# Attention on one core: the maximum and the bias of each head's exponential made by one two-source VectorE operation

## The chip, the cores and the metric

The kernel runs on one core of one Trainium2 chip, as a single launch. The metric is the device time of that launch in microseconds (us); less is better. One more execution was recorded by the hardware profiler, and all rows below come from it.

## What is computed

The reference runs two blocks over 8 sequences of 128 tokens with 256 features (8 tiles of 128 tokens). A first layer has a small cross-attention and a feed-forward part with ternary weights. The second layer is a cross-attention over 16 heads of 16 features with rounded operands, and a second feed-forward part. The change lies in the second layer's cross-attention, which in the reference reads:

```
q = _fq_sym(q, axis=-1)            # per token and head: s = max|q| / 127, at least 1e-8; q = round(q / s) * s
k = _fq_sym(k, axis=-1)
v = _fq_sym(v, axis=2)
attn = jnp.einsum('bhqd,bhkd->bhqk', q, k)     # 1024 keys for each query
attn = jax.nn.softmax(attn, axis=-1)
attn = _fq_unsigned(attn, axis=-1)             # round to 255 steps of the row's largest
out = jnp.einsum('bhqk,bhkd->bhqd', attn, v)
```

Since the row's largest softmax value becomes 255, the kernel needs only exp(s * (score - max score) + ln 255), rounded to an integer, and its sum. Here `score` is the product of the rounded query integers with the keys, and `s` is that query's scale.

## The kernel before

It is written engine by engine, with semaphores by hand; the order of the work on each engine is the order of the calls in the code. The attention of the second layer is a loop over 128 units (`U = T * H`, a token tile `t` and a head `h`). In each unit `u`:

- TensorE: `scores(u)` writes 128x1024 scores to two banks of PSUM. There are three such slots, so it waits until ScalarE has done unit u-3 (`s_exp`).
- VectorE: `attention(u)` takes the negated maximum of the 1024 scores of each row into `nm`, a ring of three (L1472).
- GpSimd: `bias(u)` computes `eb = nm * sq + ln 255` on 128x1 values (L658). `sq` holds the scales of the queries.
- ScalarE: `attention(u)` runs the exponential over the same two banks with bias `eb` and scale `sq`, writes 128x1024 integers and gives their sum through its accumulator (L992).
- The integers are turned by a DMA, or for 4 heads of 16 (from the second tile on) by TensorE with a ScalarE copy (`move`, L979), and then TensorE multiplies them with the values (L2062), some 7 units later.

Between these, VectorE does work that comes once in a tile (reciprocal of the sums L1448, scaling L1453, residual L1460) and work that comes once in two tiles, the layer norm and rounding of two finished tiles (L1127 to L1274, L1464). GpSimd has other work in the same loop: layer-norm roots, `x2_bp`, `x3_b2`, and `b1_part`, 28 pieces for the feed-forward part, one behind each bias from unit 36 on. `quantise_rows` makes the integers and scales of the queries; it is called four times by `q_quant4`, twice before unit 0 and twice between units 4 and 9.

## Time and profile before

| what | value |
|---|---|
| median of 3 runs | 398.39 us (395.93 to 398.97) |
| profiled execution | 397.65 us, its span from the first to the last instruction 395.8 us |
| granted TensorE clock, mean of the profiled execution | 0.888 |
| VectorE busy | 85% of the span |
| ScalarE busy | 80% of the span |
| TensorE matmul busy | 77% of the span |
| GpSimd busy | 39% of the span |

The time of an execution and the span of its instructions differ by 1.85 us here. The shares are averages over stages with different limits; the attention lies between 151 and 343 us of the span.

### The profile page before, as it was taken

Reading aid. Unit: us, or ns where it says so; the run is one execution under the profiler, and the core shown is the slowest. Engines: PE = TensorE matmul, PEld = TensorE weight load, DVE = VectorE, ACT = ScalarE, POOL = GpSimd, SP = SyncE. Lnnn points to the kernel's source line nnn. Section 1 sums busy time; section 2 is a strip of 40 time slices with the busy share of each in tenths; the row PEclk is TensorE's granted clock in tenths of the full one; section 3 lists DMA queues with packets and bytes.
Section 4 is the critical chain, followed back from the end, with each engine's and each line's share of the span. In section 5 each row is a group of like instructions: output and inputs, shape, how many; then the busy total and the mean of one; then the engine's idle time right before and its main releaser. Section 6 shows DMA issues by size and latency. Waiting matters only on the chain.

```text
span 395.8 us, 7466 instructions
## 1 busy us (share of the span) xinstructions
PE 304.7 (77%) x2557; PEld 190.7 (48%) x2589; DVE 334.7 (85%) x542; ACT 316.8 (80%) x517; POOL 153.9 (39%) x324
## 2 busy tenths in 40 slices
PE   7989999767696996667677768666767757777966
PEld 6656565422585883333444434434444434433433
DVE  4648998868788879878998999999999999598786
ACT  3766789967345688788999989999999999887852
POOL 6423525469740423104224565413122233156330
PEclk9969999899699899865998988999899998985578
DMA  8900013500300015959999998999898988600001
GB/s 265 393 3 3 0 61 104 208 2 0 106 0 2 1 27 104 136 106 162 181 167 166 169 166 140 161 174 172 161 173 141 170 122 153 101 0 17 13 27 55
DMA packets 126342, 42.68 MB, mean 108 GB/s; under 512 B 121056, under 2 KB 124768, under 8 KB 125536
## 3 DMA queue, kind: packets, MB, share of 16 engines
q1 hardware_dynamic: 125872, 41.60, 54.4%
q8 instruction: 21, 0.34, 0.4%
q0 software_dynamic: 144, 0.52, 0.3%
q14 instruction: 17, 0.14, 0.1%
q10 hardware_dynamic: 288, 0.07, 0.1%
HBM read 11.24 MB, written 1.05 MB: 31 GB/s over the span
## 4 chain that ended last, share of the span: by engine, by line
PE 33%; DVE 21%; ACT 21%; issue 16%; POOL 6%; DMA 1%; SPq 0%; ACTq 0%; DVEq 0%; POOLq 0%
ACT rb L992 15%; PE ps L2035 4%; DVE nm L1472 4%; PE ps L1940 4%; PE ps L2140 3%; PE ps L1944 2%; PE ps L2047 2%; PE ps L2097 2%; PE ps L2011 2%; PE ps L1913 2%; DVE st L1127 1%; PE ps L2106 1%; PE ps L2095 1%; POOL ra L558 1%; POOL ra L559 1%
## 5 line engine op out<-in xcount | busy, mean ns | idle before, releaser
L1472 DVE TENSOR_REDUCE nm<-ps 128x1 f32<-128x1024 f32 x128 | 153.3, 1218 | 11.5 <-PE ps L2035 10.8
L992 ACT ACTIVATE rb<-ps,eb,sq 128x1024 int16<-128x1024 f32 x128 | 153.6, 1212 | 9.3 <-POOL eb L658 8.7
L2035 PE MATMUL ps<-ra,rb 128*128 128x512 bf16 x229 | 80.0, 426 | 49.1 <-ACT rb L992 46.7
L658 POOL TENSOR_SCALAR eb<-nm,sq 128x1 f32<-128x1 f32 x128 | 34.2, 267 | 120.0 <-DVE nm L1472 118.9
L2035 PEld LDWEIGHTS ps<-ra,rb 128*128 128x128 bf16 x256 | 16.1, 101 | 63.6 <-ACT rb L992 60.9
L2062 PEld LDWEIGHTS ps<-ra,tern 128*128 128x128 f16 x624 | 25.5, 98 | 17.9 <-issue 7.2
L2062 PE MATMUL ps<-ra,tern 128*128 128x16 f16 x624 | 25.9, 171 | 2.7 <-DVE rb L1202 2.7
L992 ACT ACTIVATION_READ_ACCUMULATOR rb<-ps,eb,sq 128x1 f32 x128 | 26.7, 209 | 0.0
L2047 PEld LDWEIGHTS ps<-idh,rb 128*128 128x128 f16 x224 | 15.9, 107 | 14.5 <-issue 10.4
L2047 PE MATMUL ps<-idh,rb 128*128 128x128 f16 x224 | 19.3, 236 | 3.6 <-issue 2.2
L1913 PE MATMUL ps<-xqT,tern 128*128 128x512 bf16 x62 | 16.6, 397 | 6.3 <-DVE rb L1382 4.9
L2062 PEld LDWEIGHTS ps<-ra,stage 128*128 128x128 f16 x400 | 16.5, 98 | 10.1 <-issue 3.8
L1940 PE MATMUL ps<-h,ra 128*128 128x256 f32 x64 | 16.8, 429 | 3.4 <-POOL ra L559 3.4
L855 ACT ACTIVATE sB<-ps,shift,small 128x1024 uint8<-128x1024 f32 x8 | 9.7, 1208 | 9.1 <-DVE small L1420 9.0
L2062 PE MATMUL ps<-ra,stage 128*128 128x16 f16 x400 | 16.7, 171 | 0.0
L1940 PEld LDWEIGHTS ps<-h,ra 128*128 128x128 f32 x64 | 13.8, 219 | 5.7 <-issue 3.4
L1372 DVE TENSOR_TENSOR gs<-ps,sB 128x512 f32<-128x512 f32 x16 | 11.0, 688 | 6.1 <-PE ps L1913 4.4
L848 ACT ACTIVATE sl<-gs 128x512 f32<-128x512 f32 x16 | 9.8, 624 | 7.2 <-DVE rb L1382 5.7
L1418 DVE TENSOR_REDUCE small<-ps 128x1 f32<-128x1024 f32 x8 | 9.8, 1221 | 5.5 <-PE ps L1940 3.0
L599 POOL TENSOR_SCALAR small<-small 128x1 f32<-128x1 f32 x8 | 6.5, 811 | 20.2 <-DVE small L1420 20.2
L775 ACT ACTIVATE wint<-stage,wrec 128x2048 int16<-128x2048 f32 x5 | 10.0, 1998 | 5.3 <-DVE tern L1235 4.3
L1913 PEld LDWEIGHTS ps<-xqT,tern 128*128 128x128 bf16 x64 | 5.5, 100 | 15.5 <-DVE rb L1382 7.5
(242 smaller groups left out, 716.6 us busy)
## 6 DMA issues: line engine op xcount, KB each, us to landing
stage<-w SPq DMA_DIRECT2D x2, 1024.0 KB, 6.7
rb<-ra SPq DMA_DIRECT2D x16, 128.0 KB, 3.1
xs<-x SPq DMA_DIRECT2D x4, 256.0 KB, 4.2
cx<-ctx_in SPq DMA_DIRECT2D x4, 256.0 KB, 4.4
stage<-w_gate SPq DMA_DIRECT2D x1, 1024.0 KB, 7.9
stage<-w_up SPq DMA_DIRECT2D x1, 1024.0 KB, 11.1
stage<-w_down SPq DMA_DIRECT2D x1, 1024.0 KB, 4.8
cx<-wide_rows SPq DMA_DIRECT2D x1, 1024.0 KB, 6.4
```

What stands on the lines that cost most here:

```text
L658: nc.gpsimd.tensor_scalar(eb[:, u % 3:u % 3 + 1], nm[:, u % 3:u % 3 + 1], sq[:, t, h:h + 1], LN255, ALU.mult, ALU.add).then_inc(s_bias, 1)
L775: A(wint[:, :], wslot(i), ACT.Identity, scale=wrec[:, i:i + 1]).then_inc(w_int, 1)
L848: A(sl[:, n % 2, :], gs[:, n % 2, :], ACT.Silu).then_inc(g_silu, 1)
L992: A(esc[u % E_RING], bank(2 * (u % 3), 2), ACT.Exp, bias=eb[:, u % 3:u % 3 + 1], scale=sq[:, t, h:h + 1], accum_out=es[:, t % 2, h:h + 1]) ...
L1372: V.tensor_tensor(gs[:, n % 2, :], bank(GATE_UP_BANKS[n][0]), sB[:, 512 * hf:512 * hf + 512], ALU.mult).then_inc(g_scaled, 1)
L1472: V.tensor_reduce(nm[:, u % 3:u % 3 + 1], bank(2 * (u % 3), 2), AX.X, ALU.max, negate=True).then_inc(s_max, 1)
L1913: ins = M(bank(b), tern[:, w, F * k + P * c:F * k + P * c + P], xqT[:, k, 512 * hf:512 * hf + 512], start=(k == 0), stop=(k == 1))
L1940: ins = M(y[:, 2 * P * c:2 * P * c + 2 * P], m[:, 4 * k + c, :], h128[:, P * k:P * k + 2 * P], start=(k == 0), stop=(k == 1))
L2035: ins = M(bank(2 * (u % 3) + hf), qz[t % 2][:, h // 2, h % 2, :], kT[:, h // 2, 512 * hf:512 * hf + 512], start=True, stop=True)
L2047: ins = TR(half_bank(7)[:, P * c:P * c + P], esc[u % E_RING].bitcast(F16)[:, P * c:P * c + P], idh[:, :])
L2062: ins = M(bank(6)[:, HD * h:HD * h + HD], rT[u % R_RING][:, P * c:P * c + P], vq[:, c, HD * h:HD * h + HD], start=(c == 0), stop=(c == T - 1))
L2140: ins = M(b, fT16[:, t % 2, P * c:P * c + P], w[:, D * c:D * c + D], start=False, stop=(c == FC - 1))
```

## The change

One VectorE operation with two sources and an accumulator takes the place of the maximum on VectorE and the step on GpSimd. It computes (score - ln 255 / s) * (-s) for every score, writes these 1024 values as bf16 to memory that nothing reads (`unread`, three places in free buffers), and keeps their minimum, which is -s * max + ln 255: the bias itself. The two per-row numbers that it needs, `sqn = -s` and `sql = -ln 255 / s`, come from `quantise_rows`, which makes them for each query. The second source is `sql` broadcast along the row. `eb` becomes a ring of four, and VectorE waits for the exponential of unit u-4 before it writes it. The semaphore `s_max` and the tile `nm` go.

```diff
-            def bias(u):
-                t, h = divmod(u, H)
-                pool.wait_ge(s_max, u + 1)
-
-                nc.gpsimd.tensor_scalar(eb[:, u % 3:u % 3 + 1], nm[:, u % 3:u % 3 + 1], sq[:, t, h:h + 1],
-                                        LN255, ALU.mult, ALU.add).then_inc(s_bias, 1)
-
             for u in range(U + 3):
-                if u < U:
-                    bias(u)
...
-            def quantise_rows(psum, bias, factor, scale, out_i):
+            def quantise_rows(psum, bias, factor, scale, negative, shifts, out_i):
...
-                link(V.tensor_scalar(scale, ka[:, :], factor / 127.0, QMIN, ALU.mult, ALU.max))
-                link(V.reciprocal(kr[:, :], scale))
-                if factor != 1.0:
-                    link(V.tensor_scalar(kr[:, :], kr[:, :], factor, None, ALU.mult))
+                link(V.tensor_scalar(ks[:, :], ka[:, :], 1.0 / 127.0, QMIN / factor, ALU.mult, ALU.max))
+                V.tensor_scalar(scale, ks[:, :], factor, None, ALU.mult)
+                V.tensor_scalar(negative, ks[:, :], -factor, None, ALU.mult)
+                link(V.reciprocal(kr[:, :], ks[:, :]))
+                V.tensor_scalar(shifts, kr[:, :], -LN255 / factor, None, ALU.mult)
...
             def attention(u):
                 if u < U:
+                    t, h = divmod(u, H)
+                    if h == 0:
+                        dve.wait_ge(q_int, t // 2 + 1)
                     dve.wait_ge(s_ps, u + 1)
-                    if u >= 3:
-                        dve.wait_ge(s_bias, u - 2)
-                    V.tensor_reduce(nm[:, u % 3:u % 3 + 1], bank(2 * (u % 3), 2), AX.X, ALU.max,
-                                    negate=True).then_inc(s_max, 1)
+                    if u >= 4:
+                        dve.wait_ge(s_exp, u - 3)
+
+                    V.tensor_tensor_reduce(out=unread[u % 3], in0=bank(2 * (u % 3), 2), in1=sql[:, t, h:h + 1].to_broadcast([P, NK]),
+                                           scale=sqn[:, t, h:h + 1], scalar=3.0e38, op0=ALU.add, op1=ALU.min,
+                                           accum_out=eb[:, u % 4:u % 4 + 1]).then_inc(s_bias, 1)
```

VectorE's queue in the middle of the attention, around the layer norm of a finished pair of tiles, before (`nm` is the negated maximum, `ps` the scores):

```order
L1472 TENSOR_REDUCE nm<-ps 128x1 [waits s_bias,s_ps] x2
L1127 BN_STATS st<-xs 128x6 [waits x3_done]
L1127 BN_STATS st<-xs 128x6
L1130 BN_AGGR mv<-st 128x2 [waits dve_link]
L1130 BN_AGGR mv<-st 128x2
L1472 TENSOR_REDUCE nm<-ps 128x1 [waits s_bias,s_ps] x2
```

The same place after (the line numbers of the changed file differ; `stage` and `gs` are the unread outputs, `eb` the bias):

```order
L1470 ISA gs,eb<-ps,sql,sqn 128x1024 [waits s_exp,s_ps]
L1470 ISA eb 128x1
L1470 ISA stage,eb<-ps,sql,sqn 128x1024 [waits s_exp,s_ps,q_int]
L1470 ISA eb 128x1
L1120 BN_STATS st<-xs 128x6 [waits x3_done]
L1120 BN_STATS st<-xs 128x6
L1123 BN_AGGR mv<-st 128x2 [waits dve_link]
L1123 BN_AGGR mv<-st 128x2
L1470 ISA stage,eb<-ps,sql,sqn 128x1024 [waits s_exp,s_ps]
L1470 ISA eb 128x1
```

Every unit is now two instructions on VectorE: the pass over 128x1024, and a second one that writes the accumulator to `eb`. Nothing else there changed its place; VectorE's queue has 128 instructions more for the units.

GpSimd's queue from unit 32 on, where the pieces of `b1_part` (`wint`) begin, before:

```order
L658 TENSOR_SCALAR eb<-nm,sq 128x1 [waits s_max] x17
L616 TENSOR_TENSOR x<-xs,row 128x256 [waits x3_done]
L658 TENSOR_SCALAR eb<-nm,sq 128x1 [waits s_max] x3
L625 CAST wint<-wkvs 128x256 [waits w_tern,ld_wide]
L658 TENSOR_SCALAR eb<-nm,sq 128x1 [waits s_max,pool_link]
L627 TENSOR_SCALAR wint<-wint,col 128x256
L658 TENSOR_SCALAR eb<-nm,sq 128x1 [waits s_max,pool_link]
L629 TENSOR_TENSOR wint<-wkvs,wint 128x256
```

A later stretch of the same work after:

```order
L627 CAST wint<-wkvs 128x256 [waits w_tern,ld_wide]
L629 TENSOR_SCALAR wint<-wint,col 128x256 [waits pool_link]
L631 TENSOR_TENSOR wint<-wkvs,wint 128x256 [waits pool_link]
L633 CAST wint<-wint 128x256 [waits pool_link]
L629 TENSOR_SCALAR wint<-wint,col 128x256 [waits pool_link]
L471 TENSOR_SCALAR ve<-mv 128x2 [waits ln_stats,pool_link]
L472 TENSOR_TENSOR rstd<-ve,mhalf 128x2 [waits pool_link]
```

The biases no longer stand between the pieces, so each piece follows the one ahead of it as soon as that is done. The queues of TensorE and ScalarE are the same before and after, instruction by instruction and wait by wait.

VectorE's `quantise_rows` (one of four calls), before:

```order
L1194 TENSOR_TENSOR rb<-ps,row 128x512 [waits q_four,q_ps]
L1197 TENSOR_REDUCE ka<-rb 128x32 [waits dve_link]
L1198 TENSOR_SCALAR sq<-ka 128x32 [waits dve_link]
L1199 RECIPROCAL kr<-sq 128x32 [waits dve_link]
L1201 TENSOR_SCALAR kr<-kr 128x32 [waits dve_link]
L1202 TENSOR_TENSOR rb<-rb,kr 128x512 [waits dve_link]
```

And after:

```order
L1187 TENSOR_TENSOR rb<-ps,row 128x512 [waits q_four,q_ps]
L1190 TENSOR_REDUCE ka<-rb 128x32 [waits dve_link]
L1191 TENSOR_SCALAR ks<-ka 128x32 [waits dve_link]
L1192 TENSOR_SCALAR sq<-ks 128x32 [waits dve_link]
L1193 TENSOR_SCALAR sqn<-ks 128x32
L1194 RECIPROCAL kr<-ks 128x32
L1195 TENSOR_SCALAR sql<-kr 128x32 [waits dve_link]
L1196 TENSOR_TENSOR rb<-rb,kr 128x512
```

Two small instructions come in, and two of the waits on the engine's own last result go.

## Rows read from the trace of the kernel before

**Rows 1.** The page: span, and busy time of each engine.

```profile
span 395.8 us, 7466 instructions
PE 304.7 (77%) x2557; PEld 190.7 (48%) x2589; DVE 334.7 (85%) x542; ACT 316.8 (80%) x517; POOL 153.9 (39%) x324
```

**Rows 2.** The page's costliest groups: the four steps of a unit.

```profile
L1472 DVE TENSOR_REDUCE nm<-ps 128x1 f32<-128x1024 f32 x128 | 153.3, 1218 | 11.5 <-PE ps L2035 10.8
L992 ACT ACTIVATE rb<-ps,eb,sq 128x1024 int16<-128x1024 f32 x128 | 153.6, 1212 | 9.3 <-POOL eb L658 8.7
L2035 PE MATMUL ps<-ra,rb 128*128 128x512 bf16 x229 | 80.0, 426 | 49.1 <-ACT rb L992 46.7
L658 POOL TENSOR_SCALAR eb<-nm,sq 128x1 f32<-128x1 f32 x128 | 34.2, 267 | 120.0 <-DVE nm L1472 118.9
L992 ACT ACTIVATION_READ_ACCUMULATOR rb<-ps,eb,sq 128x1 f32 x128 | 26.7, 209 | 0.0
```

**Rows 3.** Timeline of VectorE: the reciprocals behind units 19 and 115.

```profile
187.80 0.24 DVE L1448 RECIPROCAL er<-es 128x16 f32<-128x16 f32 x1
...
322.36 0.24 DVE L1448 RECIPROCAL er<-es 128x16 f32<-128x16 f32 x1
```

**Rows 4.** Busy time by stretch: units 0-19, 20-115, two single tiles, the rest.

```profile
core 0: us, PE busy (x) PEld busy (x) DVE busy (x) ACT busy (x) POOL busy (x), PEclk, DMA share, GB/s
151.35:187.80 36.45, 24.81 (x174) 13.33 (x176) 30.62 (x38) 31.25 (x49) 9.72 (x28) 0.74 0.80 129
187.80:322.36 134.56, 95.86 (x1187) 59.30 (x1207) 126.33 (x148) 129.64 (x223) 47.04 (x136) 0.94 0.99 164
233.25:255.17 21.92, 16.79 (x191) 9.72 (x192) 21.22 (x28) 21.38 (x38) 11.88 (x30) 0.84 0.91 156
255.17:277.85 22.68, 15.30 (x205) 9.70 (x209) 21.08 (x26) 21.92 (x38) 5.91 (x19) 1.00 1.09 174
322.36:343.10 20.74, 14.58 (x189) 9.12 (x189) 18.57 (x29) 19.51 (x33) 5.56 (x20) 0.92 0.89 141
```

**Rows 5.** Timeline of ScalarE, two units in a row without a wait.

```profile
201.80 1.20 ACT L992 ACTIVATE rb<-ps,eb,sq 128x1024 int16<-128x1024 f32 x1
202.89 0.19 ACT L992 ACTIVATION_READ_ACCUMULATOR rb<-ps,eb,sq 128x1 f32 x1
202.99 1.20 ACT L992 ACTIVATE rb<-ps,eb,sq 128x1024 int16<-128x1024 f32 x1
```

**Rows 6.** Timeline of VectorE, a reduction and its successor; a pair of tiny instructions.

```profile
235.35 1.22 DVE L1472 TENSOR_REDUCE nm<-ps 128x1 f32<-128x1024 f32 x1
236.49 0.61 DVE L1268 TENSOR_SCALAR xqi<-xn,small 128x256 int16<-128x256 f32 x2
...
228.48 0.25 DVE L1130 BATCH_NORM_AGGREGATE mv<-st 128x2 f32<-128x6 f32 x2
```

**Rows 7.** Groups of VectorE by form: two sources, with and without a per-row scalar.

```profile
L1372 DVE TENSOR_TENSOR gs<-ps,sB 128x512 f32<-128x512 f32 x16 | 11.0, 688 | 6.1 <-PE ps L1913 4.4 <-ACT sl L848 1.7
L1186 DVE SCALAR_TENSOR_TENSOR x<-ps,col,xc 128x512 f32<-128x512 f32 x4 | 3.0, 744 | 0.0
L1577 DVE SCALAR_TENSOR_TENSOR ra<-rb,small,cx 128x1024 f32<-128x1024 f32 x8 | 10.3, 1284 | 0.7 <-POOL small L688 0.5
L1394 DVE TENSOR_TENSOR rb<-rb 128x2048 f32<-128x2048 f32 x3 | 6.9, 2285 | 0.0
L1130 DVE BATCH_NORM_AGGREGATE mv<-st 128x2 f32<-128x6 f32 x32 | 4.0, 165 | 0.6
L1201 DVE TENSOR_SCALAR kr<-kr 128x32 f32<-128x32 f32 x4 | 0.7, 182 | 0.1
```

**Rows 8.** Timeline of all engines, a bias that stands behind other work on GpSimd.

```profile
229.76 0.72 POOL L629 TENSOR_TENSOR wint<-wint 128x256 f32<-128x256 f32 x1
...
230.58 0.26 POOL L658 TENSOR_SCALAR eb<-nm,sq 128x1 f32<-128x1 f32 x1
...
230.88 1.20 ACT L992 ACTIVATE rb<-ps,eb,sq 128x1024 int16<-128x1024 f32 x1 [1.33 <-POOL eb L658]
```

**Rows 9.** Waits between 151.35 and 343.10 us: total, times, longest.

```profile
POOL eb L658 <- DVE nm L1472: 118.9, 117, 5.5
...
DVE nm L1472 <- PE ps L2035: 10.8, 32, 0.8
...
ACT rb L992 <- POOL eb L658: 8.7, 16, 2.1
```

More of the change, by code:

```diff
@@ L267, in build @@
         sq = sb("sq", [P, T, H])
+        sqn = sb("sqn", [P, T, H])
+        sql = sb("sql", [P, T, H])
         va = sb("va", [P, 3, 2])
-        nm = sb("nm", [P, 3])
-        eb = sb("eb", [P, 3])
+        eb = sb("eb", [P, 4])
+        unread = [stage[:, 0, F:F + HF].bitcast(BF16), stage[:, 0, F + HF:2 * F].bitcast(BF16), gs[:, 1, :].bitcast(BF16)]
         es = sb("es", [P, 2, H])
@@ L341, in build @@
         q_turned = [k_three, k_hat]
-        s_ps, s_max, s_bias, s_exp, s_tr, s_moved, s_av = (
-            sem(n) for n in ("s_ps", "s_max", "s_bias", "s_exp", "s_tr", "s_moved", "s_av"))
+        s_ps, s_bias, s_exp, s_tr, s_moved, s_av = (
+            sem(n) for n in ("s_ps", "s_bias", "s_exp", "s_tr", "s_moved", "s_av"))
         s_turned = [sem(f"s_turned{b}") for b in range(R_RING)]
@@ L991, in attention @@
                         act.wait_ge(o_norm, t - 1)
-                    A(esc[u % E_RING], bank(2 * (u % 3), 2), ACT.Exp, bias=eb[:, u % 3:u % 3 + 1], scale=sq[:, t, h:h + 1],
+                    A(esc[u % E_RING], bank(2 * (u % 3), 2), ACT.Exp, bias=eb[:, u % 4:u % 4 + 1], scale=sq[:, t, h:h + 1],
                       accum_out=es[:, t % 2, h:h + 1]).then_inc(s_exp, 1)
@@ L1432, in q_quant4 @@
                     dve.wait_ge(q_four, 2 * j)
-                quantise_rows(bank(Q_BANK), rowv["bq"], 0.25, sq[:, 2 * j:2 * j + 2, :].rearrange("p t h -> p (t h)"),
-                              ki).then_inc(q_int, 1)
+                of_pair = (v[:, 2 * j:2 * j + 2, :].rearrange("p t h -> p (t h)") for v in (sq, sqn, sql))
+                quantise_rows(bank(Q_BANK), rowv["bq"], 0.25, *of_pair, ki).then_inc(q_int, 1)
             def scale_wp():
```

## The prediction, made before the changed kernel was run

> **What bounds the kernel now.** I read the page's busy shares first [rows 1]: VectorE is busiest with 85%, ScalarE has 80%. Then the costliest groups [rows 2], of which the reader should see that the two longest, VectorE's maximum and ScalarE's exponential, are almost equal (153.3 and 153.6 us) and are the two passes over the same 1024 scores. GpSimd's bias takes 34.2 us, but GpSimd waits 120.0 us for VectorE in between, so its share of work bounds nothing.
>
> Next comes the stretch. The reciprocals behind units 19 and 115 [rows 3] mark off 20 units, then 96 units (six tiles), then the last 12. In the middle stretch of 134.56 us VectorE is busy for 126.33 us and ScalarE for 129.64 us [rows 4]: 8.2 and 4.9 us of slack, so a unit takes 1.40 us and both engines are within 7% of being full. That is the view the prediction rests on. A kernel with two nearly full engines gains little from a shorter hop between them and loses almost all that is added to either.
>
> The waits say the same [rows 9]: in the whole attention ScalarE waits 8.7 us for a bias, VectorE 10.8 us for scores, and the scores wait mostly for the exponentials of the ring of three slots [rows 2].
>
> **The change part by part.** *The hop through GpSimd goes.* A bias takes 0.267 us [rows 2] and sometimes stands behind a piece of other work: one at 230.58 us started right behind an instruction of 0.72 us, and the exponential behind it came 1.33 us late [rows 8]. All of ScalarE's waits for a bias are 8.7 us [rows 9]; that is the most the hop can give while ScalarE stays the later engine, and a part of it is VectorE's own lateness. Where VectorE is the later engine, an exponential that starts 0.3 us earlier frees its slot earlier, but VectorE has no use for it. I count 0.3 us, for the last unit alone.
>
> *The pass over the scores.* The reduction takes 1.218 us [rows 2] and its successor starts 1.14 us after it (235.35 to 236.49) [rows 6]: the end of one overlaps the next by 0.08 us. Two-source instructions go at the same rate: 512 elements from PSUM in 0.688 us and 2048 in 2.285 us [rows 7], 1.04 ns an element, so 1024 would take 1.22 us. The per-row scalar costs extra: 0.744 against 0.688 us at 512 elements, and 1.284 us at 1024 [rows 7]. I take 1.284 us, 0.065 us more than now; the lower bound is nothing more. A pass over fewer elements isn't in sight, so I exclude a gain.
>
> *The accumulator read.* VectorE has no such instruction in the trace of before. ScalarE has: its row reads 0.209 us [rows 2], but what it costs is the step from its start to the next instruction's, 0.10 us (202.89 to 202.99) [rows 5]. Tiny VectorE instructions behind each other step by 0.25 - 0.165 = 0.085 us [rows 6, 7]. I take 0.085 us, the same engine's row; the upper bound is the full row of 0.209 us, if nothing of it overlaps.
>
> Together a unit costs VectorE 0.15 us more; the ends are 0.085 and 0.275 us.
>
> The Trainium skill, Vector Engine (DVE) Microarchitecture Reference, section Points that are easy to get wrong, says that a scalar-tensor-tensor shape with two non-bf16 sources in SBUF runs at half throughput, since no read port is left for the accumulator. Here one source lies in PSUM, and the instruction of L1577 with two fp32 SBUF sources, without accumulator, shows no halving (1.284 us for 1024 elements); whether the accumulator brings it no row of before shows. It is the third rival below. The skill's page VectorE: DVE Perf Modes, section Two Vector instructions with no wait between them, counts an accumulator output as a second instruction that is held back until the first has finished only where start partitions differ; by it the overlap that I assume would stand.
>
> *The sum over six tiles.* VectorE's work becomes 126.33 + 96 x 0.15 = 140.7 us, above ScalarE's 129.64, and above it in single tiles too (21.22 + 2.4 = 23.6 against 21.38; 21.08 + 2.4 = 23.5 against 21.92) [rows 4]. So VectorE is the bound everywhere, and the ring of three slots (score 0.43 x 2, pass 1.28, read 0.1, exponential 1.2, some 0.2 for semaphores: 3.6 us) stays under three units of VectorE (3 x 1.46 = 4.4 us). Of the 8.2 us of slack I leave 1.5. 140.7 + 1.5 - 134.56 = +7.7 us.
>
> *The first 20 units.* 20 x 0.15 = 3.0 us. The stretch has 5.8 us in which VectorE is idle [rows 4], but partly for the projections of later queries; I take 0.8 off. Two of the four `quantise_rows` lie in it. Each gets two small instructions of 0.182 us [rows 7] that overlap, and loses two waits on its own result: +0.1 us each. Sum +2.4 us. The other two calls lie before: +0.2 us.
>
> *The last 12 units.* 12 x 0.15 = 1.8, less 0.4 of idle time that fills: +1.4 us.
>
> *What costs nothing.* The writes of 2 KB a row to unread memory ride in the pass; the added wait for unit u-4's exponential is already met when the scores of unit u exist, since TensorE waited for unit u-3. Behind it on VectorE stands only the next unit. GpSimd's 28 pieces run in a bunch; they are hidden under the scores and leave its roots for the layer norm earlier than now. No DMA moves in any queue.
>
> Total: 7.7 + 2.4 + 0.2 + 1.4 - 0.3 = +11.4 us. Against the profiled execution's own 397.65 us that is 409.0 us; its distance to the median of 398.39 us, 0.74 us, is small beside the bounds. **Forecast: 409 us, slower.**
>
> **The rivals.** *First, the hop is what counts (faster).* If the accumulator read and the scalar hide almost entirely, ScalarE becomes the only bound: 129.64 us instead of 134.56 in six tiles, and perhaps 2 us in the rest: 391 us. The place is the pair pass plus read on VectorE; the point from which it decides is 129.64 - 126.33 = 3.3 us over 96 units, 0.035 us a unit. Both nearest rows speak against it (0.065 and 0.085 us, together 0.15). For it speaks only that nothing of before shows the new instruction.
>
> *Second, it costs little (no change).* At 0.085 us a unit, VectorE's work is 126.33 + 8.2 = 134.5 us, just the present time of the stretch; with 3 us of slack left +2.9, the rest +1.2: 401.7 us. With the hop's gain it may come to 399 us.
>
> *Third, the pass runs at half rate.* 1024 x 1.04 ns = 1.07 us a unit more: 409 + 137 = 546 us. The pass would then read 2.35 us in the profile.
>
> *Fourth, the read does not overlap the pass.* If it waits for the pass to end (0.08 us) and then steps by 0.09, a unit costs 0.065 + 0.08 + 0.09 = 0.235 us: 126.33 + 22.6 + 1.5 - 134.56 = +15.9, and the other 32 units +6: about 420 us. At the upper bound of 0.275 us it is 425 us.
>
> **How the numbers follow.** About 1% (4 us) is what a measurement of this kernel can tell from no change. Forecast, 403 to 414 us: 0.51. Fourth rival, 415 to 426: 0.19. Second, 396 to 402: 0.19. First, below 394.4: 0.08. Third: 0.03. The range of 398 to 421 us holds the forecast, most of the second and of the fourth, and leaves out some 0.2. Faster by over 1% 0.08, within 1% (394.4 to 402.4 us) 0.21, slower by over 1% 0.71.
>
> **What would show it.** In the changed profile the group of the pass should read 1.28 us and the read behind it 0.15 to 0.2 us, with 0.085 us from its start to the next. VectorE should be over 97% busy between the reciprocals of units 19 and 115, that stretch some 142 us, and ScalarE's idle time there near 12 us with VectorE named as releaser; GpSimd's busy time should fall by about 34 us. VectorE's wait for scores should fall from 10.8 us to below 3. The prediction is wrong if a unit steps by less than 1.2 us on VectorE, if ScalarE remains the busiest engine, or if the last stage (343 us to the end), which the change doesn't touch, moves by more than 2 us, as a changed TensorE clock there could make it.

## The result and the profile after

| | kernel before | kernel after |
|---|---|---|
| median of 20 runs each | 396.88 us (394.87 to 401.85) | 400.45 us (397.69 to 404.31) |
| ratio after / before | | 1.007, 95% interval 1.0044 to 1.0096 |

In this comparison the change costs 0.7%, some 3 us, and not the 11.4 us (2.9%) of the forecast. The time lies inside the range of 398 to 421 us, and inside the 1% for which the prediction gave 0.21. Medians here and below are over all executions of a kernel, and ratios leave out those that were more than 1.5% slower than its fastest (2 of the 20 of after, but 7 of 12 and 5 of 10 for the kernel with the pieces spread and for the last control), so for those two the median and the ratio do not agree.

The profiled execution of after took 404.31 us, the longest of its twenty. 4.8 us of its distance to the profile of before lie ahead of the attention: the last quantising call before unit 0 starts at 150.96 us, in before at 146.13 us. In a later profile of the same kernel (the control, below; span 399.1 us) it starts at 147.04 us, so most of the 4.8 us are not the change's. Over all profiles of this document that call starts between 145.75 and 152.34 us: up to 6.6 us of difference between two executions lie ahead of the part that is changed. Stretches are compared below, not spans.

The page of after, against [rows 1]: span and busy times. GpSimd lost 34.7 us of work (153.9 to 119.2); VectorE has 136 instructions more.

```profile
span 402.5 us, 7479 instructions
PE 314.0 (78%) x2589; PEld 192.8 (48%) x2589; DVE 342.8 (85%) x678; ACT 317.3 (79%) x517; POOL 119.2 (30%) x196
```

The costliest groups of after, against [rows 2]. The pass stands in two groups by the name of its unread output; its line is L1470 now, the exponential's L985.

```profile
L985 ACT ACTIVATE rb<-ps,eb,sq 128x1024 int16<-128x1024 f32 x128 | 154.1, 1222 | 11.5 <-DVE eb L1470 10.2
...
L1470 DVE CUSTOM_DVE_ANT_0 stage<-ps,sql,sqn 128x1024 bf16<-128x1024 f32 x86 | 108.3, 1277 | 4.9 <-PE ps L2034 3.6
L1470 DVE CUSTOM_DVE_ANT_0 gs<-ps,sql,sqn 128x1024 bf16<-128x1024 f32 x42 | 53.5, 1274 | 2.3 <-PE ps L2034 1.6
```

The groups of VectorE by form hold the new second instruction of a unit, the accumulator read:

```profile
L1470 DVE DVE_READ_ACCUMULATOR2_ANT eb<- 128x1 f32 x128 | 10.6, 83 | 0.0
```

The pass reads 1.277 us, as forecast from [rows 7] (1.28), and ScalarE now waits for VectorE instead of GpSimd (11.5 us idle). The read says 0.083 us. What it costs is seen only in the timeline of VectorE, two units in a row without a wait, against [rows 6]:

```profile
231.26 1.25 DVE L1470 CUSTOM_DVE_ANT_0 stage<-ps,sql,sqn 128x1024 bf16<-128x1024 f32 x1
232.44 0.08 DVE L1470 DVE_READ_ACCUMULATOR2_ANT eb<- 128x1 f32 x1
232.44 1.28 DVE L1470 CUSTOM_DVE_ANT_0 gs<-ps,sql,sqn 128x1024 bf16<-128x1024 f32 x1
233.64 0.08 DVE L1470 DVE_READ_ACCUMULATOR2_ANT eb<- 128x1 f32 x1
```

The read and the next pass start at the same moment, 232.44, and the next read follows 1.20 us later. So a unit steps by 1.20 us where it stepped by 1.14, all of the addition in the pass, and nothing for the read. Over the 128 units the next instruction starts 1.202 us behind the pass on average; three reductions of before in a row (189.86 to 193.27) step by 1.137 us. The difference is 0.065 us.

Waits of after between 150 and 345 us, against [rows 9]. ScalarE waits for its bias about as long as before (9.8 against 8.7 us). VectorE waits for scores for 3.6 + 1.6 = 5.2 us, half of the 10.8 before, but not the 3 of the forecast.

```profile
ACT rb L985 <- DVE eb L1470: 9.8, 16, 1.8
...
DVE stage L1470 <- PE ps L2034: 3.6, 11, 0.8
...
DVE gs L1470 <- PE ps L2034: 1.6, 3, 0.8
```

Busy time of after in the stretches of [rows 4]: units 0 to 19, then the six tiles one by one, then the last 12 units. The last three columns are the granted TensorE clock, the DMA share and GB/s.

```profile
150.96:191.12 40.16, 28.10 (x225) 16.21 (x223) 36.36 (x76) 35.56 (x54) 6.27 (x11) 0.86 0.78 128
191.12:212.12 21.00, 16.51 (x204) 9.77 (x203) 20.27 (x36) 20.95 (x38) 5.53 (x11) 0.93 1.09 180
212.12:235.65 23.53, 16.99 (x220) 10.39 (x218) 22.46 (x45) 22.30 (x39) 4.95 (x11) 0.98 1.11 172
235.65:260.73 25.08, 20.09 (x189) 10.75 (x190) 23.64 (x43) 21.64 (x36) 6.90 (x13) 0.68 0.76 133
260.73:283.57 22.84, 15.92 (x211) 9.59 (x208) 21.98 (x42) 22.01 (x39) 1.58 (x3) 1.00 1.13 177
283.57:305.76 22.19, 15.23 (x189) 8.87 (x190) 21.88 (x43) 21.21 (x37) 0.72 (x1) 1.00 0.94 153
305.76:328.60 22.84, 15.93 (x211) 9.60 (x208) 21.98 (x42) 22.01 (x39) 1.58 (x3) 1.00 0.90 154
328.60:350.59 21.99, 16.12 (x182) 9.40 (x182) 19.36 (x42) 19.36 (x32) 2.12 (x7) 0.84 0.80 132
```

Three things are to be seen. The fourth tile (260.73) answers to the one at 255.17 before: VectorE's work grew by 0.90 us there (21.08 to 21.98) and the tile by 0.16 us (22.68 to 22.84), since VectorE had 1.6 us to spare and has 0.86. The third tile (235.65) is the costly one: 25.08 us against 21.92, with 23.64 us of VectorE work against 21.22, and the granted clock at 0.68. And the first stretch, from the same quantising instruction, takes 40.16 us; before it took 41.67 us (146.13 to 187.80). In all: first stretch -1.5, six tiles +2.9 (134.56 to 137.48), last 12 units +1.3 (20.74 to 21.99), the rest -0.8 (52.70 to 51.91): +1.9 us from that instruction to the end.

### The profile page after: what moved, and what is told of

The parts are those of the page before. It is cut to its first block and busy times, and to the rows that moved or that the text cites. A ratio compares the mean times of both kernels' runs of the same rounds, so it can differ in the third digit from the quotient of the medians.

```text
span 402.5 us, 7479 instructions
## 1 busy us (share of the span) xinstructions
PE 314.0 (78%) x2589; PEld 192.8 (48%) x2589; DVE 342.8 (85%) x678; ACT 317.3 (79%) x517; POOL 119.2 (30%) x196
## 3 DMA queue, kind: packets, MB, share of 16 engines
HBM read 11.24 MB, written 1.05 MB: 31 GB/s over the span
## 5 line engine op out<-in xcount | busy, mean ns | idle before, releaser
L985 ACT ACTIVATE rb<-ps,eb,sq 128x1024 int16<-128x1024 f32 x128 | 154.1, 1222 | 11.5 <-DVE eb L1470 10.2
L2034 PE MATMUL ps<-ra,rb 128*128 128x512 bf16 x256 | 86.0, 421 | 43.6 <-ACT rb L985 42.6
L1470 DVE CUSTOM_DVE_ANT_0 stage<-ps,sql,sqn 128x1024 bf16<-128x1024 f32 x86 | 108.3, 1277 | 4.9 <-PE ps L2034 3.6
L1470 DVE CUSTOM_DVE_ANT_0 gs<-ps,sql,sqn 128x1024 bf16<-128x1024 f32 x42 | 53.5, 1274 | 2.3 <-PE ps L2034 1.6
L618 POOL TENSOR_TENSOR x<-xs,row 128x256 f32<-128x256 f32 x8 | 5.8, 726 | 85.4 <-DVE xs L1454 85.4
L985 ACT ACTIVATION_READ_ACCUMULATOR rb<-ps,eb,sq 128x1 f32 x128 | 27.9, 218 | 0.0
L2046 PE MATMUL ps<-idh,rb 128*128 128x128 f16 x224 | 18.1, 226 | 6.5 <-ACT rb L985 5.4
L471 POOL TENSOR_SCALAR ve<-mv 128x2 f32<-128x2 f32 x7 | 1.5, 210 | 71.4 <-DVE mv L1123 71.4
L2046 PEld LDWEIGHTS ps<-idh,rb 128*128 128x128 f16 x224 | 14.7, 101 | 16.4 <-ACT rb L985 8.4
```

The lines of the kernel that those rows point to most:

```text
L985: A(esc[u % E_RING], bank(2 * (u % 3), 2), ACT.Exp, bias=eb[:, u % 4:u % 4 + 1], scale=sq[:, t, h:h + 1], accum_out=es[:, t % 2, h:h + 1]) ...
L1470: V.tensor_tensor_reduce(out=unread[u % 3], in0=bank(2 * (u % 3), 2), in1=sql[:, t, h:h + 1].to_broadcast([P, NK]), scale=sqn[:, t, h:h + ...
L2034: ins = M(bank(2 * (u % 3) + hf), qz[t % 2][:, h // 2, h % 2, :], kT[:, h // 2, 512 * hf:512 * hf + 512], start=True, stop=True)
L2046: ins = TR(half_bank(7)[:, P * c:P * c + P], esc[u % E_RING].bitcast(F16)[:, P * c:P * c + P], idh[:, :])
```

## The experiments

Below, "the attention" is the time from that quantising instruction to the reciprocal behind the last unit: 41.67 + 134.56 + 20.74 = 197.0 us before, 199.6 us after. Each such stretch is read from one execution. Ratios are to the kernel before, run on the same chip with the kernels of the same group; there are four groups.

**The reduction without the hop.** The reduction of before is put back and its result goes straight to `eb`; ScalarE waits for it as after, and GpSimd has no step. The exponential takes constants as bias and factor, so the scaled bias is left out; so it is in the kernels with the fixed factor and without the read.

```diff
-   V.tensor_tensor_reduce(out=unread[u % 3], in0=bank(...), in1=sql..., scale=sqn..., ..., accum_out=eb[:, u % 4:u % 4 + 1])
+   V.tensor_reduce(eb[:, u % 4:u % 4 + 1], bank(2 * (u % 3), 2), AX.X, ALU.max, negate=True)
```

> The changed kernel with the plain maximum in place of the two-source pass; its result signals ScalarE directly. The exponential takes a constant bias and a constant tiny factor, so the scaled bias is left out. It has the gain of the hop alone. Theory A (the pass costs 0.065 us a unit through its per-row factor, the accumulator read costs nothing, and the hop gives 2 to 3 us back): the reduction steps by 1.14 us, and the time is 3 us below before, about 394 us. Rival B (the hop gives nothing while both engines are nearly full): as before, 397 us.

Measured: 396.84 us beside 397.68 us of before, ratio 0.9992 (0.9954 to 1.0031). With the hop gone and nothing added to VectorE, the kernel is as fast as before. The hop alone is worth nothing that can be measured (the interval allows 1.8 us of gain); the rival by which ScalarE would become the only bound and give 391 us falls. GpSimd's pieces run in a bunch here too, which adds to VectorE's work in the third tile (22.69 us, before 21.22), so what is measured is the hop together with that.

**GpSimd's pieces spread again.** The kernel after, with GpSimd waiting once a unit for the bias, so that its pieces of `b1_part` no longer run in a bunch.

```diff
+   if u < U:
+       pool.wait_ge(s_bias, u + 1)
```

> The changed kernel, in which GpSimd waits for each unit's bias again without working on it, so that the 28 pieces for the feed-forward part are spread over units as before. Theory A, with the bunch of pieces slowing VectorE's small instructions beside it (0.49 against 0.16 us, 1.08 against 0.61 us, 0.72 against 0.29 us in one tile): about 1 us less than the changed kernel, 399.5 us, and those instructions back at their short durations. Rival: GpSimd's order is hidden, 400.5 us.

Measured: 400.03 us, ratio 1.0006 (0.9957 to 1.0056). After was not run in this group, so the total can't tell this kernel from before or from after. What its trace shows is below, with the point on the bunch.

**A fixed factor in the pass.** `scale` is the number -0.25 instead of the per-row `sqn`; the accumulator read stays.

```diff
-   scale=sqn[:, t, h:h + 1], scalar=3.0e38, op0=ALU.add, op1=ALU.min,
+   scale=-0.25, scalar=3.0e38, op0=ALU.add, op1=ALU.min,
```

> The changed kernel with the constant -0.25 in place of the per-row factor sqn in the two-source pass; bias and factor of the exponential are constants, so the scaled bias is left out. The accumulator is still read. Theory A (the whole added 0.065 us is the per-row factor): the pass reads 1.22 us and steps by 1.14 us, the time is as in the kernel with the plain reduction and no hop, about 394 us. Rival C (two sources or the accumulator make it slow): 1.28 us and the changed kernel's 400.5 us.

Timeline of VectorE of this kernel, three units without a wait:

```profile
288.18 1.21 DVE L1472 CUSTOM_DVE_ANT_0 stage<-ps,sql 128x1024 bf16<-128x1024 f32 x1
289.32 0.08 DVE L1472 DVE_READ_ACCUMULATOR2_ANT eb<- 128x1 f32 x1
289.32 1.22 DVE L1472 CUSTOM_DVE_ANT_0 gs<-ps,sql 128x1024 bf16<-128x1024 f32 x1
290.46 0.08 DVE L1472 DVE_READ_ACCUMULATOR2_ANT eb<- 128x1 f32 x1
290.46 1.22 DVE L1472 CUSTOM_DVE_ANT_0 stage<-ps,sql 128x1024 bf16<-128x1024 f32 x1
```

The step is 1.14 us, that of the one-source reduction [rows 6]. Averaged over all units the next instruction starts 1.143 us behind the pass, in after 1.202 us. So a second source, a 2 KB output and the read cost VectorE less than 0.01 us together; the per-row factor is the rest, 0.06 us. Measured 396.74 us, ratio 0.997 (0.9932 to 1.0008), as without the hop.

**No read.** The pass without an accumulator output.

```diff
-   accum_out=eb[:, u % 4:u % 4 + 1]).then_inc(s_bias, 1)
+   accum_out=None).then_inc(s_bias, 1)
```

> The changed kernel without the accumulator read; bias and factor of the exponential are constants, so the bias is left out. Theory A (the read overlaps wholly): pass and step stay 1.28 and 1.205 us, the time stays at 400 us. Rival D (the read costs its share although its row overlaps): the step falls and the time goes to 397 us or below.

Timeline of VectorE of this kernel:

```profile
289.75 1.28 DVE L1472 CUSTOM_DVE_ANT_0 stage<-ps,sql,sqn 128x1024 bf16<-128x1024 f32 x1
290.95 1.28 DVE L1472 CUSTOM_DVE_ANT_0 gs<-ps,sql,sqn 128x1024 bf16<-128x1024 f32 x1
```

The step is 1.20 us without the read as with it. Measured 399.15 us, ratio 1.0031 (0.999 to 1.0073), between before and after. Its attention takes 200.1 us, that of after 199.6. So the read costs nothing that shows, in the timeline or in the stretch; the total alone, with an interval that reaches from before to after, would not decide it.

**The pass and the hop.** The pass writes `nm`, and GpSimd copies it to `eb` in its old place.

```diff
+   if u < U:
+       pool.wait_ge(s_max, u + 1)
+       nc.gpsimd.tensor_scalar(eb[:, u % 4:u % 4 + 1], nm[:, u % 4:u % 4 + 1], ones[:, 0:1], 0.0, ALU.mult, ALU.add).then_inc(s_bias, 1)
...
-   accum_out=eb[:, u % 4:u % 4 + 1]).then_inc(s_bias, 1)
+   accum_out=nm[:, u % 4:u % 4 + 1]).then_inc(s_max, 1)
```

> The changed kernel with the hop put back: the two-source pass writes to nm, and GpSimd carries it to eb with an instruction of the old form, behind each of which one of its other pieces stands as before. It has the cost of the pass without the gain of the hop. If the hop is worth what the stretches of the two profiles say (1.5 us in the first 20 units, some 0.5 us a light tile), the time is 3 us over the changed kernel, about 403 us (ratio 1.015). Rival B, after the kernel with the plain reduction and no hop showed no gain: the hop is worth nothing, 400.5 us (ratio 1.007 to 1.009).

Measured 403.14 us beside 396.16 of before, ratio 1.0186 (1.0136 to 1.0237). The control of the same chip, the kernel after once more:

> The changed kernel again, unchanged, as a control beside the other three on the same chip. Expected ratio 1.007, as in the 20 runs of it.

Measured 401.58 us, ratio 1.0158 (1.0103 to 1.0214): more than the 1.007 of the first comparison, with intervals that do not meet. Against the control the hop costs 1.6 us, within the overlap of the two intervals.

**The change for the first 20 units only.** From unit 20 on, the reduction and GpSimd's bias of before.

```diff
+   if u < 20:
        V.tensor_tensor_reduce(...)        # the pass, as after
+   else:
+       V.tensor_reduce(nm[:, u % 4:u % 4 + 1], bank(2 * (u % 3), 2), AX.X, ALU.max, negate=True).then_inc(s_max, 1)
```

> The two-source pass only for units 0 to 19, where the profile after took 1.5 us less than before; from unit 20 on the plain maximum and the bias on GpSimd, as before. Nothing is left out. Theory A: 1 to 1.5 us below before (ratio 0.997). Rival: the first stretch is paid back later by the clock or by the ring, ratio 1.000.

Measured 397.71 us, ratio 1.0032 (0.999 to 1.0073). The first stretch takes 40.26 us, 1.4 less than before, but the whole gains nothing. The first stretches of all profiles fall in two groups: with the hop 41.3 to 41.9 us (five kernels); without it, at a step of up to 1.20 us, 39.7 to 40.3 us (eleven). The closest pair is the pass with the hop and the pass without: 41.92 against 40.16 us. So there the hop is worth 1 to 2 us, or what goes with it: TensorE's granted clock is lower in all five with the hop (0.77 to 0.84 against 0.86 and 0.87), and no run separates the two. The six tiles behind it took 136.8 us in this profile, before 134.6, so nothing of it reached the end; where those 2.2 us lie is seen further below.

**More VectorE work.** A tiny instruction (128x2) behind each unit of the kernel after; three of them (128x1); and one behind each unit of the kernel before.

```diff
+   V.tensor_scalar(spare[:, u, :], idf[:, 0:2], 2.0, None, ALU.mult)
```

> The changed kernel with one more instruction of 128x2 on VectorE behind each unit's pass and read, which steps by the 0.085 us that the prediction charged for the accumulator read. Theory A (the prediction's chain from VectorE's time to the kernel's was right and only the read was mis-sized, the slack being used up): 0.085 x 128 = 10.9 us, most of it seen: 408 us or more (ratio 1.027). Rival E (VectorE isn't the bound even now, a unit's time is set by ScalarE and the ring): 2 us or less, ratio 1.012 or below.

> The changed kernel with three tiny instructions (128x1) on VectorE behind each unit's pass and read, about 0.07 + 2 x 0.09 = 0.25 us a unit. Theory A (VectorE is the bound from the changed kernel's load on, and what is added counts fully once the slack is gone): 0.18 x 128 = 23 us over the kernel with one such instruction, about 425 us (ratio 1.07). Rival E (the bound lies elsewhere): less than 1.05.

> The kernel before, with one more instruction of 128x2 on VectorE behind each unit's maximum: the step that cost 0.07 us a unit in the changed kernel, almost what the two-source pass adds (0.065 us), with reduction, bias and GpSimd as before. Theory A (the pass is nothing but 0.065 us more of VectorE's time): the same as the changed kernel with the hop put back, ratio 1.013 to 1.018. Rival (the pass costs by something else too, its writes or its second source): 1.008 or less here.

Timeline of VectorE, the kernel before with one tiny instruction:

```profile
302.14 1.22 DVE L1473 TENSOR_REDUCE nm<-ps 128x1 f32<-128x1024 f32 x1
303.27 0.16 DVE L1475 TENSOR_SCALAR spare<-idf 128x2 f32<-128x2 f32 x1
303.34 1.22 DVE L1473 TENSOR_REDUCE nm<-ps 128x1 f32<-128x1024 f32 x1
```

Here the unit steps by 1.20 us, as in the kernel after: 401.52 us, ratio 1.008 (1.004 to 1.0119). That is the edge of the rival by which the pass costs by something else too (1.008 or less), below the 1.013 to 1.018 expected. But those figures came from the group in which after stood at 1.016; in the first comparison it stood at 1.007, and it was not run in this group. So the total doesn't decide whether the pass has another effect; its time on VectorE and the six tiles (137.4 and 137.5 us) show none.

One tiny instruction on top of the pass (step 1.275 us) gives 403.11 us, ratio 1.0202 (1.0157 to 1.0246). It fits neither of the cases on record (408 us or more, 1.012 or less): beside its control, 401.58 us, the 9 us of work added (0.07 x 128) show as 1.5 us. Three of them (step 1.39 us) give 412.62 us, ratio 1.035 (1.0292 to 1.0408), below the 425 us, and below the 1.05 under which VectorE was not to be the bound; its busy share below says that it is. They step by 0.19 us and not by 0.25; that takes 8 us off the 425, and the rest of the miss is that 14.7 us of work more than with one extra show as 9.5.

Busy time in the fourth and fifth tile of the kernel with one extra, and in the same two of that with three:

```profile
257.13:280.79 23.66, 15.50 (x209) 9.69 (x210) 23.40 (x61) 22.00 (x39) 1.58 (x3) 1.00 1.10 173
280.79:304.01 23.22, 15.92 (x192) 9.40 (x194) 22.99 (x60) 21.73 (x36) 0.73 (x1) 0.85 0.82 145
```

```profile
264.05:289.25 25.20, 18.12 (x196) 10.90 (x201) 24.55 (x92) 22.50 (x40) 1.58 (x3) 0.83 1.02 158
289.25:314.55 25.30, 19.11 (x195) 10.98 (x196) 24.88 (x93) 22.41 (x37) 0.73 (x1) 0.70 0.77 135
```

VectorE is 97 to 99% busy in all four, at granted clocks from 0.70 to 1.00. Set against each other, the six tiles of the kernels read:

| kernel | step of a unit, us | VectorE busy, us | six tiles, us | slack, us |
|---|---|---|---|---|
| before [rows 4] | 1.14 | 126.3 | 134.6 | 8.2 |
| reduction without hop | 1.14 | 126.8 | 136.3 | 9.5 |
| first 20 units only | 1.14 | 126.2 | 136.8 | 10.6 |
| fixed factor | 1.14 | 127.5 | 135.7 | 8.2 |
| before with one extra | 1.20 | 131.5 | 137.4 | 6.0 |
| after | 1.20 | 132.2 | 137.5 | 5.3 |
| after, two controls | 1.20 | 132.8, 132.8 | 140.2, 140.2 | 7.4, 7.5 |
| pieces spread | 1.20 | 131.2 | 137.5 | 6.4 |
| no read | 1.20 | 131.6 | 139.8 | 8.1 |
| pass and hop | 1.20 | 131.8 | 139.1 | 7.3 |
| after with one extra | 1.275 | 138.5 | 140.6 | 2.1 |
| after with three extra | 1.39 | 147.2 | 148.7 | 1.5 |

The slack is used up gradually. From the kernels with a step of 1.14 us to those with 1.20 us, where VectorE and ScalarE are equally full, VectorE's work grows by some 5 us and the tiles by some 3 (means of four and of seven profiles); from there to one extra, 6.6 us more show as 1.8; from 138 us of work on (one extra to three) 8.7 us show as 8.1. Kernels of one load still differ by up to 3 us, so the first two figures are rough.

**Half of the value products.** Those differences lie in tiles in which TensorE's clock was granted at half for a stretch. If its amount of work set their length, halving the products with the values (4 key blocks of 8) should shorten them. Done to the kernels after and before:

```diff
-   for c in range(T):
+   for c in range(T // 2):
```

> The changed kernel in which the products with the values take only 4 of 8 key blocks: half of that multiplication is left out, some 2.9 us of TensorE's time in a tile of 16 units. Scores, passes, exponentials and turns are whole. Theory F (where TensorE's clock is granted at half, TensorE sets the unit's time, and that is the slack VectorE keeps): the tiles with a halved clock fall from 24 or 25 us to below 23 us, the clean ones stay at 22.2 and 22.8, and the time falls by 3 us or more, to 397 us. Rival: no tile moves, 400 us.

> The kernel before with the same half of the products with the values left out. Theory F: its tiles with a halved clock get shorter too, some 3 us less than before (393 us); the difference to the changed kernel with the same left out is then VectorE's alone, 3 to 5 us. Rival: 397 us.

The fifth tile of the control, and that of the kernel after with half of the products:

```profile
280.66:304.66 24.00, 16.83 (x186) 10.03 (x190) 22.22 (x43) 21.55 (x37) 0.73 (x1) 0.86 0.82 142
```

```profile
281.47:305.50 24.03, 15.56 (x126) 8.49 (x130) 22.21 (x43) 21.54 (x37) 0.73 (x1) 0.86 0.77 142
```

60 matmuls fewer, and the tile is as long. Measured 401.67 us, ratio 1.0089 (1.0051 to 1.0127), for after and 400.81 us, 1.0039 (0.9999 to 1.0079), for before: no faster than with all products. At clock 1.00 the same tile takes 22.19 us (the fifth of after, above), so the tile with a stretch at half is 1.8 us longer. TensorE's busy time in it falls by only 1.27 us (16.83 to 15.56), not by the 2.9 expected, so the test is a weaker one; the value products are not what delays the tile.

**The projection ahead of the scores.** Timeline of TensorE in the control, inside that stretch (granted clock 0.50, that is 1.2 GHz, from 290 to 296 us):

```profile
292.91 1.20 PE L2075 MATMUL ps<-wps,rb 128*128 128x256 f32 x2
293.90 1.06 PE L2034 MATMUL ps<-ra,rb 128*128 128x512 bf16 x2
294.75 0.41 PE L2061 MATMUL ps<-ra,stage 128*128 128x16 f16 x8
295.01 1.20 PE L2075 MATMUL ps<-wps,rb 128*128 128x256 f32 x2
```

One round of scores (0.85 us from start to start), value products (0.26) and half of the tile's fp32 projection (1.00) takes 2.1 us, where VectorE needs 1.2. TensorE has no gap, and the next two passes wait 0.81 and 0.44 us for scores. So this place was tested: the projection made cheap (four bf16 products of a constant matrix) in the kernels after and before, and made double in the kernel after, beside another control.

```diff
-   ins = M(bank(7)[:, D:2 * D], oT[:, t % 2, k, :], wps[:, k, :], start=(k == 0), stop=(k == 1))
+   for hf in range(2):          # cheap; double: the old product twice
+       ins = M(bank(7)[:, D + P * hf:D + P * hf + P], idb[:, :], idb[:, :], start=True, stop=True)
```

> The kernel after, with the output projection of a tile (two fp32 products of 128x256, which stand between scores in TensorE's queue) replaced by four bf16 products of 128x128 of a constant matrix, so the result of the projection is left out. In the control's fifth tile, at half the TensorE clock, a unit took 2.1 us for two units: scores 0.85, value products 0.26, one projection product 1.0 us, with TensorE busy without a gap while VectorE waited 0.81 and 0.44 us for scores. If the projection in TensorE's queue is what makes the tiles with a halved stretch long, such a tile falls from about 24.0 to 22.5 us or less, the six tiles to 138 us or less, and the ratio to before to 1.000 to 1.006. If the delay comes from elsewhere in the halved stretch, tiles of 24 to 25 us at 0.75 to 0.86 remain and the time is the control's.

> The same replacement in the kernel before; the result of the projection is left out. It shows what the projection is worth without the change. If VectorE's slack of 8.2 us over six tiles already absorbs it, 0 to 1 us less than before; the comparison with the same edit on the kernel after shows the price of the change where the projection no longer stands before the scores: I expect after to be 1 to 2 us slower still.

> The kernel after with each projection product issued twice (the result of the projection is changed). It adds some 0.8 us of TensorE's work a tile at full clock and 2 us at half. If the projection ahead of the scores is the delay, a tile with a halved stretch grows by 1 to 2 us to 25 to 26 us, and the whole by 3 to 8 us; if the tiles' length comes from elsewhere, the time stays within 1 us of the control's.

> The kernel after once more, on the same chip as the two with the replaced projection: 1.007 to 1.016 of before.

The last expectation, of a control at 1.007 to 1.016, was missed too, at 1.0002. Third and fourth tile of the kernel after with the cheap projection, then the same two with the double one:

```profile
233.00:257.09 24.09, 17.21 (x195) 9.67 (x197) 23.56 (x43) 21.53 (x36) 6.93 (x13) 0.75 0.84 138
257.09:279.93 22.84, 14.66 (x207) 9.16 (x208) 21.98 (x42) 22.01 (x39) 1.58 (x3) 1.00 1.01 175
```

```profile
240.14:266.34 26.20, 18.88 (x189) 11.19 (x194) 23.66 (x45) 21.64 (x36) 6.93 (x13) 0.80 0.73 127
266.34:289.93 23.59, 16.04 (x212) 10.45 (x212) 22.15 (x42) 22.30 (x39) 1.58 (x3) 1.00 1.02 172
```

| kernel | median, us | ratio | third tile (clock) | fourth tile (clock) |
|---|---|---|---|---|
| after, control | 399.28 | 1.0002 (0.9956 to 1.0048) | 24.80 (0.76) | 22.85 (1.00) |
| after, cheap | 402.01 | 1.0123 (1.0013 to 1.0234) | 24.09 (0.75) | 22.84 (1.00) |
| after, double | 408.47 | 1.0299 (1.0226 to 1.0372) | 26.20 (0.80) | 23.59 (1.00) |
| before, cheap | 400.56 | 1.0111 (1.0069 to 1.0154) | 21.92 (0.93) | 22.69 (1.00) |

Cheap and double rest on 4 executions each. Double, it costs 9 us beside the control, more than the 3 to 8 expected, and 0.75 us in a tile even at full clock. Cheap, it gives 0.7 us in the tile with the halved stretch, nothing at full clock, and nothing in the whole: 402.01 us beside the control's 399.28, and in the kernel before 1.1% more than before, where 0 to 1 us less was expected. In that profile the six tiles take 135.0 us (before 134.6) and the last quantising call starts 4.2 us later than in before; why the kernel is slower isn't shown.

The traces say more about the halved stretches. A tile has its projection 11 to 16 us behind its start. In the profiles of after, of its two controls and of the kernel with the pieces spread, a tile is long where the first product of the projection runs at half clock (1.20 us) and short where it runs at full clock. The fifth tile of after has a short one (granted clock 1.00):

```profile
295.39 0.68 PE L2075 MATMUL ps<-wps,rb 128*128 128x256 f32 x2
```

| stretch | projection at full clock | at half clock | at half clock, but cheap |
|---|---|---|---|
| first tile, us | 21.00 (after) | 22.23, 22.22 (controls), 22.16 (spread) | 21.38 |
| fifth tile, us | 22.19 (after), 22.18 (spread) | 24.00, 24.00 (controls) | |
| last 12 units, us | 20.36, 20.38 (controls) | 21.99 (after), 22.06 (spread) | 20.75 |

After had its clock halved at the start of its first tile (191 to 193 us) and has the short one; the controls had it at the projection (the first of them from 198 to 200 us) and are 1.2 us longer. With the projection cheap, and the clock halved at the same place, most of that is gone: 0.85 of 1.2 us in the first tile, 1.2 of 1.6 us in the last 12 units. So at these two places the projection is most of what a halved stretch costs, and in the third tile the third seen above. It is not all: the second tile of the kernel after with the cheap projection has a halved stretch behind its projection (224 to 227 us) and takes 24.25 us, the control's 23.51.

The same is seen with the step of before: its third tile has its clock halved from 234 to 240 us, ahead of the projection, and takes 21.92 us, as long as in the kernel before with the cheap projection; where the stretch took in the projection (the first 20 units only, 243 to 249 us) it takes 23.67. That tile (+1.75) and the first (+0.72, again at its projection) are where this kernel lost its 2.2 us. So over half of the 3.2 us by which the third tile of after is longer than that of before goes with the projection at half clock, and not with VectorE's pass.

In the five profiles of kernels with the hop none or one of the seven projections has its first product at half clock, in the three of after two or three. Whether taking the hop away moves the halved stretches there isn't shown; it is one execution each.

The control stands at 1.0002 in this group. The same two kernels thus came at 1.007, 1.016 and 1.000 (medians +3.6, +5.4 and +1.8 us): the change costs 0 to 1.6%, and differences below 1% between kernels rest on little.

## Why the prediction was wrong

**The step that failed is the accumulator read.** It was charged at 0.085 us a unit, the step of tiny VectorE instructions, and ScalarE's own read with its 0.10 us stood beside it [rows 5]. On VectorE the read starts together with the next instruction and costs nothing; without it nothing changes. That was 0.085 x 128 = 10.9 us of the 19.2 us of work added, and it is what made the forecast large. The prediction had named the sign of it, 0.085 us from the read's start to the next instruction, and the trace shows 0.00. The same forecast with the read at nothing would be 126.33 + 96 x 0.065 + 1.5 - 134.56 = -0.5 us for the six tiles, and with +0.7, +0.2, +0.4 and -0.3 for the rest about +0.5 us. That is 1 to 5 us below what the three comparisons gave (+1.8, +3.6, +5.4).

**The slack was mis-sized for the true load.** 1.5 us was left of 8.2. Near the load that I had forecast this holds: the kernel with one extra instruction has 138.5 us of work and 2.1 us of slack, and at +0.135 us a unit its ratio is 1.020, some 8 us, where +11.4 was forecast at +0.15. That is weak support, since after itself stood at 1.016 in that group. At the true load 5.3 to 8.1 us stay. In after the fourth and the sixth tile keep 0.86 us each, with ScalarE as full as VectorE there (22.01 and 21.98), and the third, with the halved clock, keeps 1.4; the controls keep 2.1 to 2.2 us more, in the tiles whose projection ran at half clock. "VectorE is the bound everywhere" was wrong with it, and so was "loses almost all that is added to either".

**The GpSimd pieces were costed at nothing.** Where they run in a bunch, VectorE's small instructions on SBUF take longer. Timeline of VectorE in the kernel after, in its third tile beside the bunch, each with the piece of GpSimd that overlaps it, and in its fifth tile without the bunch:

```profile
237.29 0.72 POOL L631 TENSOR_TENSOR wint<-wint 128x256 f32<-128x256 f32 x1
237.55 0.49 DVE L1249 TENSOR_SCALAR small<-small 128x2 f32<-128x2 f32 x1
...
239.40 1.08 DVE L1262 TENSOR_SCALAR xqi<-xn,small 128x256 int16<-128x256 f32 x2
239.48 0.85 POOL L631 TENSOR_TENSOR wint<-wkvs,wint 128x256 f32<-128x256 f32 x1
...
241.45 0.72 POOL L631 TENSOR_TENSOR wint<-wint 128x256 f32<-128x256 f32 x1
241.60 0.72 DVE L1268 TENSOR_SCALAR stage<-xqi 128x512 bf16<-128x512 int16 x1
...
285.48 0.17 DVE L1249 TENSOR_SCALAR small<-small 128x2 f32<-128x2 f32 x1
...
287.01 0.61 DVE L1262 TENSOR_SCALAR xqi<-xn,small 128x256 int16<-128x256 f32 x2
...
288.74 0.29 DVE L1268 TENSOR_SCALAR stage<-xqi 128x512 bf16<-128x512 int16 x1
```

The third tile of the kernel with the pieces spread shows the other side:

```profile
233.12:257.05 23.93, 17.55 (x196) 10.35 (x197) 22.36 (x43) 21.53 (x36) 7.58 (x14) 0.82 0.82 140
```

The three instructions take 0.16, 0.76 and 0.28 us there, and VectorE's work is 22.36 us, 23.64 in after and 23.57 in the control: the bunch adds 1.2 us in one tile. That it moves the total isn't shown.

**The first 20 units** were forecast at +2.4 us and came at -1.5. The added work did not show, and the stretch without the hop, costed at 0.3 us for the last unit alone, is 1 to 2 us shorter. VectorE is busy for only 36.4 of its 40.2 us in this stretch, so there a bias that comes sooner can show; that this is the reason and not the clock is argued, not tested. The two `quantise_rows` grew by 0.05 us each, from first to last start (2.27 to 2.32), where 0.1 was forecast; four of their five waits for VectorE's own last result stay, so one goes and not the two named ahead of the prediction. The last 12 units came at +1.3 (forecast +1.4) in after and at -0.4 in both controls: the +1.3 is luck, since there the projection ran at half clock.

**What held.** The per-row factor: 0.065 us, by the pass and by the fixed factor. The second source and the output at nothing. GpSimd's busy time, -34.7 us against -34; ScalarE's idle time, 11.5 against 12 with VectorE named. The pass does not run at half rate: 1.277 us against 2.35. The rule of the Trainium skill (Vector Engine (DVE) Microarchitecture Reference, section Points that are easy to get wrong) speaks of two non-bf16 sources in SBUF; with one of them in PSUM, as here, no halving shows. The Trainium skill's page VectorE: DVE Perf Modes, section Two Vector instructions with no wait between them, counts an accumulator output as a second instruction, held back only for differing start partitions. The trace agrees for the instruction behind the read, which starts with it, 0.00 us of delay. Of the rivals, the second (it costs little) had the size of the result, with a step of 0.065 instead of 0.085 us. That the time lies in the range owes something to luck: the read was put 10.9 us too high and the slack some 4 to 7 us too low, which pull opposite ways.

**What stays open.** Why three comparisons of the same two kernels differ by 1.6%. Where the stretches of halved clock fall differs between profiles of one kernel, and a tile whose projection they meet was 1.2 to 1.8 us longer; the time ahead of the attention differs by several microseconds as well. Either could make that difference, but no run here sets them, and what decides where the clock falls isn't shown. No kernel tried is faster than before by more than its interval.

## What to carry to other kernels

An instruction's row in the profile is not its price: read the distance between the starts of neighbours, and take that of the same engine, since ScalarE's accumulator read costs 0.10 us here and VectorE's nothing. Where two engines are both nearly full, price an addition by how full the other one is: here a third to a half of it showed while they were level, nearly all of it in the six tiles once one was clearly ahead, and removing a third engine's short step between them brings little. Before two tiles are compared, look whether the same instruction ran at the same granted clock in both. When the cost rests on an operation that the trace does not have, keep a forecast with that term at zero as a case of its own, with more than a small chance.

## What the runs showed of the hardware

- VectorE's accumulator read, row 0.083 us, costs no time: the next instruction starts with it (step 1.20 us with and without). A per-row factor costs 0.06 us an instruction (step 1.20 against 1.14 us with a number); a second source broadcast along the row and a bf16 output of 128x1024 cost less than 0.01 us.
- Small VectorE instructions on SBUF take 0.49, 1.08 and 0.72 us beside back-to-back GpSimd work, 0.16, 0.76 and 0.28 us at the same place with that work spread, and 0.17, 0.61 and 0.29 us without it. The passes over PSUM at the same place are not slowed (1.27 us).
- TensorE's clock was granted at half (1.2 GHz) for stretches of 2 to 20 us inside the attention (235 to 251 us in after, right behind a tile at 0.98; 176 to 196 us in before with the cheap projection), at other places in another profile of the same kernel: its fifth tile had 1.00 and 22.19 us in one, 0.86 and 24.00 us in the other; with nearly full VectorE (three extra) such tiles differ little, 25.20 us at 0.83 and 25.30 at 0.70.
- A halved stretch costs by where it falls: 1.2 to 1.8 us where the tile's fp32 projection runs in it (a product 1.20 instead of 0.68 us, ahead of the scores), nothing seen at the start of a tile (after, 191 to 193 us; before, 234 to 240 us).
